# Hybrid attention and feed-forward block: pairs of projection pieces on 64-row halves of TensorE, a new order of pieces, three banks for them

## Chip, cores and metric

The kernel runs on one core of one Trainium2 chip. The metric is the device time of one launch in microseconds (us), lower is better. Times of single instructions come from one profiled execution.

## The reference

x has 8 batches of 1024 tokens with 256 features. Both branches start from the normalised x, and the output is x plus both:

```python
xn = _layernorm(x, axis=-1)
# attention branch: 16 heads of 16
x_proj = silu(xn @ W1 + b1)
u, v, q, k = split(x_proj, 4, axis=-1)
scores = einsum("bqhd,bkhd->bhqk", qh, kh)
attn = silu(scores) / S
av = einsum("bhqk,bkhd->bqhd", attn, vh).reshape(B, S, D)
y = layernorm(av * u, gamma, beta) @ W2 + b2
# feed-forward branch, ternary weights
h = layer_norm(xn, ln1_g, ln1_b) @ ternary(w1).T + b1
h = layer_norm(gelu(h), ln2_g, ln2_b)
out = h @ ternary(w2).T + b2
x = x + y + out
```

There is no softmax: each score only goes through silu, so ScalarE evaluates 8 x 16 x 1024 x 1024 of them.

## The kernel before

**Blocks, groups, rounds.** A batch is a block (b = 0 to 7). Its attention is cut into 64 groups: 2 halves c of the heads, 2 halves h of the query tokens, 2 interleaved sets o of heads, 8 tiles t of keys. A group is four score products (`scores`, line 1079), each of 64 rows and 512 columns; two of them at a time stand on the two row halves of the array. ScalarE turns a group into attn in two Silu instructions of 128x1024 (line 636), and TensorE multiplies attn by V (`times_v`, line 1101, four column tiles of 32, each fp32 product in two passes, so 8 matmul records a group). Two groups make a round; a block has 32 rounds. The text calls the 16 matmul records of line 1101 in a round "the AV products"; a round is counted from the start of its AV products to the start of the next.

**What TensorE does in a round** (`body`, line 1222): the four scores of group 2n; the AV products of the two groups before; the four scores of group 2n+1; then the pieces that the table gives the round. The first scores of a half group wait for the Silu of the same half of the group before, since there is one set of four score banks.

**Pieces.** All other TensorE work is cut into pieces, each filling one PSUM bank: `xt` (transposes of normalised x), `k`, `q`, `u` (projections, 6 matmuls of 128x512, line 1136; fp32r high and low parts), `v` (12 of 128x256), `f1.t.half` (first feed-forward product, 4 of 128x512, line 1154), `g.t.half` (4 transposes of the hidden rows, line 1163), `f2.t` (second product, 16 of 128x256, line 1170), `zt` (8 transposes in a pair of pieces, line 1180) and `a` (12 of 128x256, line 1186) for the end of the attention branch. VectorE or ScalarE empties the bank. Steps with no TensorE work stand in the same table: `gelu` (ScalarE, line 681, with a table load before and after), `ln2`, `nrm2`, `y`, `px`, `zs`, `ln1`, `xn` (VectorE), `vs` (ScalarE).

**Order.** Every engine walks the same hand-written `TABLE`, one row per group, two rows per round (line 61 and below); `LAST_ROUNDS` replaces rounds 19 to 31 in the last block. xt, k.0, q.0 and v in a row are for the next block, zt, zs and a for the one before. Pieces take the two banks `FP` in turn (`bank_of`, `turn_of`). The AV products add up in one of two banks `OP`, which change every 16 groups; VectorE reads a full one in `output` (line 831). In block 0, TensorE also computes constants (`setup_step`, line 1190) in `OP[:, 1]`.

**f2 after g.** f2.t waits with its first eight matmuls for the split of g.t.0 on VectorE (lines 917, 922 and 924), and with the other eight for g.t.1.

Of the kernel before, what the change touches and what calls it, by code (L numbers as in the profile page):

```python
# [128 lines left out]
def parsed(row):  # L129
# [9 lines left out]
    19: "ln2.2 f2.2",  # L139
# [4 lines left out]
    24: "g.5.0",  # L144
    25: "g.5.1 gelu.3 f2.5 zs.0 zt.0 zt.1",
    26: "ln2.3 a.0",
    27: "nrm2.3 g.6.0 zs.1",
    28: "g.6.1 a.1",
    29: "f2.6",
    30: "g.7.0 g.7.1",  # L150
# [75 lines left out]
def bank_of(x, step):  # L226
    return PLACE[x, step] % 2


def turn_of(x, step):  # L230
    return PLACE[x, step] // 2 + 1


def hybrid_block_kernel(nc, x, W1, b1, b1c, W2, b2, gamc, betc, l1gc, l1bc, w1T, fb1, l2gc, l2bc, w2T, fb2, out):
# [6 lines left out]
    with ctx:  # L241
# [1096 lines left out]
```

## Time and profile before

| | us |
|---|---|
| median of 3 runs | 1492.84 |
| lowest and highest | 1492.25, 1493.19 |
| the profiled execution, whole | 1493.36 |
| its span in the trace | 1491.6 |
| TensorE busy | 1464.8 (98%) |
| ScalarE busy | 1208.9 (81%) |
| VectorE busy | 895.3 (60%) |

The 1.8 us between the span and the whole lie around the span. Busy TensorE means that some matmul is in flight, not that columns stream. So the length of a round is read from starts of matmuls, and compared with what its pieces need.

### The profile page before, as it was taken

The numbers are of one execution on the slowest core, as the hardware profiler recorded it, in microseconds if no ns is written. First come the engines' busy times: TensorE is split into PE (matmuls) and PEld (weight loads), VectorE is DVE, ScalarE is ACT, GpSimd is POOL, SyncE is SP. The second block draws the span as 40 slices with busy tenths as digits, with TensorE's granted clock in tenths as the row PEclk, the third lists the DMA queues.
The fourth block names the chain that finished last, engine by engine and source line by source line (L and its number), as shares of the span: only waits on it lengthen the run. The fifth ranks groups of instructions, "written<-read, shape, count | busy, mean of one in ns | idle before, by whom it ended". The sixth has DMA issues, their size and how long they took to land.

```text
span 1491.6 us, 25963 instructions
## 1 busy us (share of the span) xinstructions
PE 1464.8 (98%) x9942; PEld 784.7 (53%) x9942; DVE 895.3 (60%) x1719; ACT 1208.9 (81%) x1273; POOL 97.4 (7%) x197
## 2 busy tenths in 40 slices
PE   8999999999999999999999999999999999999998
PEld 7445555455554555554554455545555455554544
DVE  5557655576546854468654685447755476545745
ACT  4788888888788887887878878788788887888885
POOL 2001000010000100001000010000100001000001
PEclk9999999999999999999999999999999999999999
DMA  7351052410524106340153402443033510435100
GB/s 248 81 128 57 15 132 65 130 57 15 156 71 100 58 15 156 95 104 29 30 155 99 113 1 59 126 129 84 1 89 110 142 57 5 115 81 142 29 1 29
DMA packets 67996, 123.49 MB, mean 83 GB/s; under 512 B 12832, under 2 KB 14496, under 8 KB 66976
## 3 DMA queue, kind: packets, MB, share of 16 engines
q1 hardware_dynamic: 67712, 121.57, 29.9%
q8 instruction: 79, 1.29, 0.4%
q14 instruction: 45, 0.37, 0.1%
q10 hardware_dynamic: 160, 0.26, 0.1%
HBM read 79.84 MB, written 41.94 MB: 82 GB/s over the span
## 4 chain that ended last, share of the span: by engine, by line
PE 88%; DVE 5%; ACT 4%; issue 1%; DVEq 1%; DMA 0%; ACTq 0%
PE outs L1101 30%; PE scores L1079 22%; PE fill L1136 10%; PE fill L1170 9%; PE fill L1154 7%; PE fill L1186 3%; PE fill L1163 3%; ACT attn L636 3%; PE fill L1145 2%; DVE tmp L917 1%; PE fill L1126 1%; DVE hid L900 1%; ACT hid L681 1%; DVE st L813 1%; ACT L636 1%
## 5 line engine op out<-in xcount | busy, mean ns | idle before, releaser
L636 ACT ACTIVATE attn<-scores 128x1024 f32<-128x1024 f32 x1024 | 991.4, 1023 | 225.3 <-PE scores L1079 220.6
L1101 PE MATMUL outs<-attn,V 128*32 128x512 f32 x4096 | 494.3, 600 | 0.0
L1079 PE MATMUL scores<-QS,KS 64*128 64x512 f32 x2048 | 387.7, 452 | 8.3 <-ACT attn L636 7.0
L1079 PEld LDWEIGHTS scores<-QS,KS 64*128 64x128 f32 x2048 | 163.0, 184 | 300.4 <-ACT attn L636 241.5
L1101 PEld LDWEIGHTS outs<-attn,V 128*32 128x32 f32 x4096 | 107.2, 109 | 235.8 <-issue 235.1
L900 DVE SCALAR_TENSOR_TENSOR hid<-fill,ratq,fb1b 128x512 f32<-128x512 f32 x128 | 96.1, 751 | 77.6 <-PE fill L1154 72.3
L917 DVE TENSOR_TENSOR tmp<-fill,l2g 128x512 f32<-128x512 f32 x128 | 88.6, 692 | 88.6 <-PE fill L1163 81.1
L1170 PE MATMUL fill<-Wq,hgh 128*128 128x256 f32 x504 | 128.2, 292 | 2.0 <-DVE hgl L924 1.1
L1136 PE MATMUL fill<-xp,W1h 128*128 128x512 f32 x384 | 128.4, 416 | 0.5 <-DVE xp L949 0.5
L1170 PE MATMUL fill<-Wq,hgl 128*128 128x256 f32 x504 | 123.1, 282 | 0.0
L1170 PEld LDWEIGHTS fill<-Wq,hgh 128*128 128x128 f32 x504 | 95.8, 190 | 18.9 <-issue 14.6
L1170 PEld LDWEIGHTS fill<-Wq,hgl 128*128 128x128 f32 x504 | 96.1, 191 | 0.7
L571 POOL TENSOR_TENSOR rp<-mv,epst 128x2 f32<-128x2 f32 x64 | 12.6, 197 | 1281.7 <-DVE mv L817 907.9
L924 DVE TENSOR_TENSOR hgl<-tmp,hgh 128x512 fp32r<-128x512 f32 x128 | 88.6, 692 | 9.9 <-issue 0.4
L1136 PEld LDWEIGHTS fill<-xp,W1h 128*128 128x128 f32 x384 | 66.1, 188 | 36.7 <-issue 26.9
L1163 PE MATMUL fill<-ident,hid 128*128 128x128 f32 x512 | 78.4, 281 | 3.5 <-DVE hid L900 2.1
L813 DVE BATCH_NORM_STATS2 st<-hid 128x6 f32<-128x512 f32 x128 | 79.1, 681 | 2.9
L1136 PE MATMUL fill<-xp,W1l 128*128 128x512 f32 x192 | 75.4, 392 | 0.0
L1163 PEld LDWEIGHTS fill<-ident,hid 128*128 128x128 f32 x512 | 56.0, 141 | 35.4 <-issue 25.8
L1154 PE MATMUL fill<-Wq,yT 128*128 128x512 f32 x256 | 71.5, 408 | 1.0
L1154 PE MATMUL fill<-Wq,yX 128*128 128x512 f32 x256 | 71.8, 410 | 0.0
L681 ACT ACTIVATE hid<-hid 128x2048 f32<-128x2048 f32 x32 | 60.4, 1911 | 7.7 <-DVE hid L900 7.5
(138 smaller groups left out, 1349.3 us busy)
## 6 DMA issues: line engine op xcount, KB each, us to landing
QS<-q_scratch SPq DMA_DIRECT2D x254, 128.0 KB, 3.3
k_scratch<-kst SPq DMA_DIRECT2D x64, 256.0 KB
q_scratch<-qst SPq DMA_DIRECT2D x64, 256.0 KB
KS<-k_scratch SPq DMA_DIRECT2D x128, 128.0 KB, 3.2
KS<-k_scratch SPq DMA_DIRECT2D x256, 64.0 KB, 3.4
out_dram<-part SPq DMA_DIRECT2D x15, 512.0 KB, 2.6
xin<-in_x SPq DMA_DIRECT2D x7, 1024.0 KB, 5.1
xin<-in_x SPq DMA_DIRECT2D x2, 512.0 KB, 4.3
```

Of the source, the lines that this page charges most:

```text
L636: nc.scalar.activation(attn_of(g)[:, 2 * hf:2 * hf + 2, :], SP[:, 2 * hf:2 * hf + 2, :], ACT.Silu).then_inc(s_silu, 1)
L681: nc.scalar.activation(rows, rows, ACT.Gelu).then_inc(s_gelu, 1)
L813: V_.bn_stats(st[:, j, n, :] if len(views) > 1 else st[:, j, :], v)
L900: V_.scalar_tensor_tensor(out=hid_of(t)[:, cols], in0=FP[:, k, :], scalar=ratq[:, t:t + 1], in1=fb1b[:, cols], op0=ALU.mult, op1=ALU.add). ...
L917: V_.tensor_tensor(tmp[:, :].rearrange("p (c n) -> p c n", n=P), FP[:, k, :].rearrange("p (c n) -> p c n", n=P), l2g[:, 4 * r:4 * r + 4].u ...
L924: V_.tensor_tensor(hgl[:, r, :], tmp[:, :], hgh[:, r, :].bitcast(F32), ALU.subtract).then_inc(s_hg, 1)
L1079: ins = mm(SP[:, j, :], KS[rows, pair, t * P:(t + 1) * P], QS[rows, pair - c * PPC, h * HALF:(h + 1) * HALF], start=True, stop=True)
L1101: ins = mm(OP[32 * j:32 * j + 32, g // RUN % 2, :], V[:, t, c * HPC // 2 + j, o * DH:o * DH + 2 * DH], attn_of(g)[:, n, :], start=(o == 0 ...
L1136: ins = mm(bank.rearrange("p (i n) -> p i n", i=2), w[:, kc, col:col + P], xp[:, 2 * h:2 * h + 2, part, kc, :], start=n == 0, stop=n == le ...
L1154: ins = mm(bank, y_of(t // 2)[:, part, kc, t % 2 * P:(t % 2 + 1) * P], Wq1[:, kc, hf * HALF:(hf + 1) * HALF], start=n == 0, stop=n == len( ...
L1163: ins = nc.tensor.transpose(bank[:, n * P:(n + 1) * P], hid_of(t)[:, col:col + P], ident[:, :])
L1170: ins = mm(bank[:, 0:D], w[:, r, n * P:(n + 1) * P], Wq2[:, 4 * r + n, :], start=i == 0, stop=i == len(passes) - 1)
```

## The change

1. `paired`: when the pieces of a round are exactly one pair (k and q of one half, two u, two f1 of one tile, two g of one tile), they run on 64-row halves (`in_halves`). A 128-row matmul becomes two of 64 rows, one on each row half, at the same time for different pieces. k, q, u and f1 are `crossed`: in phase 0 the first piece uses rows 0 to 63 and the second rows 64 to 127; in phase 1 they change over and add to the same banks. Before phase 1 TensorE waits for the semaphore `first_halves_done`, which the last matmul of phase 0 raises. g in halves are transposes of 64 rows. f2 stays on the full array (`SUM_IN_HALVES = False`).
2. In such a round the first half of the next group's scores stands between phase 0 and phase 1, and the second half behind phase 1. ScalarE's Silu of the first half stands before the evacuation of the pieces, the other behind it.
3. `TABLE` and `LAST_ROUNDS` are new. Blocks 1 to 6 have six rounds in halves: 2 (k.1.0 q.1.0), 6 (u.1.0 u.0.0), 9 (k.1.1 q.1.1), 10 (f1.0.0 f1.0.1), 24 and 30 (k and q of the next block). Over the kernel there are 38 such rounds of k, q or u, 8 of f1 and 4 of g (rounds 20, 22, 27, 29 of the last block).
4. Pieces have three banks; the AV products have one (`OP`). Their first product of every 16 groups waits until VectorE has read the sum before. The constants of block 0 use the third bank of the pieces; block 0 has no pieces in its first five rounds, and k.1.0 and q.1.0 run in its round 5 (`DELAYED`).
5. f2.t whose g pieces ran in halves waits for both splits before its first matmul.

```diff
-FP = ctx.enter_context(nc.psum_tensor("fill", [P, 2, HALF], F32))
+OP = ctx.enter_context(nc.psum_tensor("outs", [P, HALF], F32))
+FP = ctx.enter_context(nc.psum_tensor("fill", [P, FILLS, HALF], F32))
...
+def paired(pieces):
+
+    kinds = [s[0] for x, s in pieces]
+    if kinds == ["f2"]:
+        return SUM_IN_HALVES
+    if len(pieces) != 2 or pieces[0][0] != pieces[1][0]:
+        return False
+    (_, one), (_, two) = pieces
+    return kinds in (["f1", "f1"], ["g", "g"]) and one[1] == two[1] or kinds == ["k", "q"] and one[1:] == two[1:] or kinds == ["u", "u"]
...
+            def crossed(steps, phase):
+
+                if phase == 0:
+                    for x, step in steps:
+                        wait_free(x, step)
+                        wait_data(x, step)
+                else:
+                    pe.wait_ge(s_half, CROSSED.index(steps[0]) + 1)
+                count = 4 if steps[0][1][0] == "f1" else 6
+                for n in range(count):
+                    for half in range(2):
+                        x, step = steps[half ^ phase]
...
+                        rows = slice(half * P // 2, (half + 1) * P // 2)
...
             def body(b):
                 for n in range(ROUNDS):
-                    scores(b, 2 * n)
+                    full, group = pieces_of(b, n)
+                    nb, ng = next_group(b, 2 * n + 1)
                     for g in (2 * n - 2, 2 * n - 1):
...
-                    scores(b, 2 * n + 1)
-                    for x, s in steps_of(b, n):
+                    for hf in range(2):
+                        scores(b, 2 * n + 1, hf)
...
+                    for x, s in full:
                         step(x, *s)
...
+                    for hf in range(2):
+                        if group:
+                            in_halves(group, hf)
+                        if nb < NB:
+                            scores(nb, ng, hf)
```

Two rows of the new table that matter, rounds 25 and 26: before, "g.5.0 | g.5.1 gelu.3 v.0 xn.3 v.1 | f2.5 | ln2.3 | xt.3 v.2" reach from round 24 to 26; now round 25 is "g.5.0 g.5.1 v.0 gelu.3 v.1 xt.2 ln2.3" and round 26 "xn.3 nrm2.3 v.2 f2.5". Likewise round 15 gives up f1.6.1 and ln2.1 to round 16.

TensorE, round 24 (in block 0), before: from the scores of the odd group to the AV products of round 25. `W1h` and `W1l` are the projection weights, `xp` the transposed x.

```order
267 L1079 MATMUL scores<-QS,KS 128x512 x4
268 L1101 MATMUL outs<-attn,V 32x512 x8
269 L1079 MATMUL scores<-QS,KS 128x512 x4
270 L1136 MATMUL fill<-xp,W1h 128x512 x2
271 L1136 MATMUL fill<-xp,W1l 128x512
272 L1136 MATMUL fill<-xp,W1h 128x512 x2
273 L1136 MATMUL fill<-xp,W1l 128x512
274 L1163 MATMUL fill<-ident,hid_61 128x128 x4
275 L1079 MATMUL scores<-QS,KS 128x512 x4
276 L1101 MATMUL outs<-attn,V 32x512 x8
```

The same round in the changed kernel.

```order
272 L1165 MATMUL outs<-attn,V 32x512 x8
273 L1147 MATMUL scores<-QS,KS 128x512 x4
274 L1216 MATMUL fill<-xp,W1h 128x512 x4
275 L1216 MATMUL fill<-xp,W1l 128x512 x2
276 L1216 MATMUL fill<-xp,W1h 128x512 x4
277 L1216 MATMUL fill<-xp,W1l 128x512 x2
278 L1147 MATMUL scores<-QS,KS 128x512 x2
279 L1216 MATMUL fill<-xp,W1h 128x512 x4
280 L1216 MATMUL fill<-xp,W1l 128x512 x2
281 L1216 MATMUL fill<-xp,W1h 128x512 x4
282 L1216 MATMUL fill<-xp,W1l 128x512 x2
283 L1147 MATMUL scores<-QS,KS 128x512 x2
```

One k piece and one g piece became a k and a q piece, 24 matmuls of 64 rows, with two scores in their middle and two at their end.

ScalarE, rounds 24 to 27 of the same block, before. Line 636 is the Silu of the scores, 681 is gelu, 662 the high part of xt, 642 evacuates k or q.

```order
47 L642 ACTIVATE kst<-fill,b1s 128x512
48 L636 ACTIVATE attn<-scores 128x1024 x4
49 L681 ACT_TABLE_LOAD
50 L681 ACTIVATE hid_62<-hid_62 128x2048
51 L636 ACT_TABLE_LOAD
52 L636 ACTIVATE attn<-scores 128x1024 x4
53 L662 ACTIVATE xp<-fill 128x512
```

The same stretch in the changed kernel.

```order
43 L685 ACTIVATE kst<-fill,b1s 128x512
44 L685 ACTIVATE qst<-fill,b1s 128x512
45 L679 ACTIVATE attn<-scores 128x1024 x3
46 L724 ACT_TABLE_LOAD
47 L724 ACTIVATE hid_62<-hid_62 128x2048
48 L705 ACTIVATE xp<-fill 128x512
49 L679 ACT_TABLE_LOAD
50 L679 ACTIVATE attn<-scores 128x1024 x8
```

xt.2 moved in between gelu.3 and the table load that brings Silu back.

TensorE, round 20 of the last block, in the changed kernel: g.3.0 and g.3.1 in halves, and behind them f2.3, whose first matmul is the row of line 1319.

```order
2814 L1165 MATMUL outs<-attn,V 32x512 x8
2815 L1147 MATMUL scores<-QS,KS 128x512 x4
2816 L1235 MATMUL fill<-ident,hid_64 128x64 x8
2817 L1147 MATMUL scores<-QS,KS 128x512 x2
2818 L1235 MATMUL fill<-ident,hid_64 128x64 x8
2819 L1147 MATMUL scores<-QS,KS 128x512 x2
2820 L1165 MATMUL outs<-attn,V 32x512 x8
2821 L1147 MATMUL scores<-QS,KS 128x512 x4
2822 L1319 MATMUL fill<-Wq_57,hgh 128x256
```

Before, the same eight transposes stood in one row, ahead of all four scores:

```order
2795 L1101 MATMUL outs<-attn,V 32x512 x8
2796 L1079 MATMUL scores<-QS,KS 128x512 x4
2797 L1163 MATMUL fill<-ident,hid_64 128x128 x8
2798 L1079 MATMUL scores<-QS,KS 128x512 x4
2799 L1101 MATMUL outs<-attn,V 32x512 x8
```

The second half of the transposes now stands behind two scores, so both g banks fill at the end of the round.

## Rows read from the trace of the kernel before

**Rows 1.** The page: busy time of each engine with its share.

```profile
PE 1464.8 (98%) x9942; PEld 784.7 (53%) x9942; DVE 895.3 (60%) x1719; ACT 1208.9 (81%) x1273; POOL 97.4 (7%) x197
```

**Rows 2.** Waits, whole kernel: who waited for whom, us, times, longest.

```profile
PEld scores L1079 <- ACT attn L636: 241.5, 348, 1.3
```

**Rows 3.** Stretches: length, busy us (count) by engine, PEclk; block 5 rounds 0-10, 11-18, 19-23, 24-31.

```profile
944.19:1001.49 57.30, 56.95 (x382) 28.86 (x380) 28.19 (x60) 48.13 (x56) 3.58 (x8) 1.00 0.38 102
1001.49:1051.08 49.59, 49.06 (x310) 25.21 (x308) 35.70 (x70) 41.89 (x40) 1.79 (x5) 1.00 0.34 87
1051.08:1077.81 26.73, 26.04 (x198) 13.97 (x196) 19.14 (x35) 20.68 (x24) 5.15 (x9) 1.00 0.01 2
1077.81:1125.15 47.34, 47.25 (x343) 27.31 (x341) 26.67 (x46) 39.41 (x44) 0.89 (x2) 1.00 0.36 99
```

**Rows 4.** Stretches: block 5 rounds 11-12, 15-16, 24-26; block 0 rounds 1-10; block 7 19-31.

```profile
1001.49:1015.61 14.12, 13.98 (x78) 6.98 (x76) 8.96 (x16) 12.30 (x12) 0.00 (x0) 1.00 0.66 153
1025.29:1041.45 16.16, 15.77 (x107) 9.60 (x105) 10.94 (x20) 13.92 (x13) 0.58 (x2) 1.00 0.44 130
1077.81:1097.15 19.34, 19.25 (x144) 11.78 (x142) 11.82 (x22) 17.31 (x19) 0.89 (x2) 1.00 0.10 28
...
38.20:95.30 57.10, 57.10 (x329) 26.39 (x327) 28.34 (x47) 43.51 (x51) 0.00 (x0) 0.96 0.37 97
...
1413.09:1480.75 67.66, 63.68 (x470) 32.25 (x468) 37.98 (x74) 53.40 (x55) 3.58 (x8) 1.00 0.02 9
```

**Rows 5.** Timeline, TensorE, block 5 round 5, u.1.1 and u.1.0: start, us, line, tiles, count.

```profile
969.10 1.92 PE L1101 MATMUL outs<-attn,V 128*32 128x512 f32 x16
970.95 0.73 PE L1079 MATMUL scores<-QS,KS 64*128 64x512 f32 x4
971.62 0.73 PE L1136 MATMUL fill<-xp,W1h 128*128 128x512 f32 x2
972.19 0.39 PE L1136 MATMUL fill<-xp,W1l 128*128 128x512 f32 x1
972.42 0.63 PE L1136 MATMUL fill<-xp,W1h 128*128 128x512 f32 x2
972.88 0.39 PE L1136 MATMUL fill<-xp,W1l 128*128 128x512 f32 x1
...
974.56 0.73 PE L1079 MATMUL scores<-QS,KS 64*128 64x512 f32 x4
```

**Rows 6.** Timeline, ScalarE, the evacuation of u.1.1 in that round.

```profile
973.33 0.69 ACT L642 ACTIVATE uz<-fill,b1s 128x512 f32<-128x512 f32 x1
```

**Rows 7.** Timeline, TensorE, block 5 round 0, then ScalarE in it.

```profile
946.04 0.73 PE L1079 MATMUL scores<-QS,KS 64*128 64x512 f32 x4
946.71 1.09 PE L1180 MATMUL fill<-ident,uz 128*128 128x128 f32 x8
...
948.58 0.49 PE L1079 MATMUL scores<-QS,KS 64*128 64x512 f32 x2 [0.35 <-ACT attn L636]
949.00 1.92 PE L1101 MATMUL outs<-attn,V 128*32 128x512 f32 x16
...
946.59 3.77 ACT L636 ACTIVATE attn<-scores 128x1024 f32<-128x1024 f32 x4 [0.48 <-PE scores L1079]
```

**Rows 8.** Timeline, ScalarE, block 5: the gelu window of round 15.

```profile
1029.65 1.28 ACT L681 ACT_TABLE_LOAD   x1
1030.95 3.71 ACT L681 ACTIVATE hid<-hid 128x2048 f32<-128x2048 f32 x2
```

**Rows 9.** Timeline, TensorE, block 5 round 21: the first matmul of f2.3, the scores behind f2.3.

```profile
1064.10 0.38 PE L1170 MATMUL fill<-Wq,hgh 128*128 128x256 f32 x1
...
1066.21 0.73 PE L1079 MATMUL scores<-QS,KS 64*128 64x512 f32 x4
```

**Rows 10.** Timeline, VectorE, round 20: the split of g.3.0, the begin of g.3.1's.

```profile
1059.59 0.69 DVE L917 TENSOR_TENSOR tmp<-fill,l2g 128x512 f32<-128x512 f32 x1 [1.35 <-PE fill L1163]
...
1061.65 0.69 DVE L917 TENSOR_TENSOR tmp<-fill,l2g 128x512 f32<-128x512 f32 x1
```

More of the change, by code:

```diff
@@ L138 @@
 LAST_ROUNDS = {
-    19: "ln2.2 f2.2",
+    19: "f2.2",
     20: "g.3.0 g.3.1 nrm2.2",
@@ L143 @@
     23: "f2.4",
[L144 to L150, printed above, removed]
+    24: "",
+    25: "g.5.0 g.5.1 gelu.3 ln2.3 zs.0 zt.0 zt.1",
+    26: "nrm2.3 f2.5 a.0",
+    27: "g.6.0 g.6.1 zs.1",
+    28: "f2.6 a.1",
+    29: "g.7.0 g.7.1",
+    30: "",
     31: "",
@@ L164 @@
 assert sorted(OPENING) == sorted(s for s in ORDER if is_next(s))
-EARLIER = {1: parsed("k.1.0")}
-MOVED = [s for n in sorted(EARLIER) for s in EARLIER[n]]
+SETUP_ROUNDS = 5
+DELAYED = [s for g in range(2 * SETUP_ROUNDS) for s in SLOTS[g] if s[0] in FILLERS and s[0] not in POST and not is_next(s)]
 def steps_of(b, n):
@@ L176, in steps_of @@
         return
-    if b == 0:
-        for s in EARLIER.get(n, ()):
-            yield b, s
+    if b == 0 and n == SETUP_ROUNDS:
+        for s in DELAYED:
+            yield 0, s
     for g in (2 * n, 2 * n + 1):
@@ L431, in last_piece @@
         def last_piece(bank):
-            return [xs for xs in PIECES if bank_of(*xs) == bank][-1]
+            return [xs for xs in PIECES if bank in [k for k, turn in BANKS[xs]]][-1]
         def last_a_tile(i, j):
@@ L730, in _ @@
                         sum_of_abs(i)
+            for hf in range(2):
+                silu_half(0, 0, hf)
+            act.wait_ge(s_const, 3)
+            step(0, "vs", 0)
             for b in range(NB):
@@ new lines, in transposed @@
+            def transposed(steps, phase):
+                if phase == 0:
+                    for x, step in steps:
+                        wait_free(x, step)
+                        wait_data(x, step)
+                for c in range(phase * HC // 2, (phase + 1) * HC // 2):
+                    for half in range(2):
+                        x, (kind, t, r) = steps[half]
+                        k = bank_of(x, (kind, t, r))
+                        toks = slice(half * P // 2, (half + 1) * P // 2)
+                        ins = nc.tensor.transpose(FP[:, k, c * P // 2:(c + 1) * P // 2], hid_of(t)[toks, c * P:(c + 1) * P],
+                                                  ident[toks, toks])
+                        if c == HC - 1:
+                            ins.then_inc(s_fill[k], 1)
@@ new lines, in summed @@
+            def summed(steps, phase):
+                (x, step), = steps
+                t = step[1]
+                if phase == 0:
+                    wait_free(x, step)
+                pe.wait_ge(s_hg, 2 * T * x + 2 * t + 2)
+                for n in range(4):
+                    for w in (hgh, hgl):
+                        for half, (k, turn) in enumerate(BANKS[x, step]):
+                            rows = slice(half * P // 2, (half + 1) * P // 2)
+                            ins = mm(FP[:, k, 0:D], w[rows, phase, n * P:(n + 1) * P], Wq2[rows, 4 * phase + n, :],
+                                     start=phase == 0 and n == 0 and w is hgh, stop=phase == 1 and n == 3 and w is hgl)
+                            if phase == 1 and n == 3 and w is hgl:
+                                ins.then_inc(s_fill[k], 1)
@@ L1110, in step, with in_halves @@
+            def in_halves(steps, phase):
+                kind = steps[0][1][0]
+                (transposed if kind == "g" else summed if kind == "f2" else crossed)(steps, phase)
             def step(x, kind, *a):
@@ L1280, in _ @@
                 step(0, *s)
+            for hf in range(2):
+                scores(0, 0, hf)
             for b in range(NB):
                 body(b)
-            pe.wait_ge(s_z, DC * NH * (NB - 1) + 3)
+            wait_evacuated(pe, *last_piece(2))
             last_hidden(0)
```

308 lines of the change are left out of this document (193 added, 115 removed).

## The prediction

> **What bounds the kernel now.** The busy times come first: TensorE 98%, ScalarE 81%, VectorE 60% [rows 1]. A busy TensorE only has a matmul in flight, so next comes who waits. TensorE's weight loads for the scores wait 348 times for a Silu, 241.5 us in all, mostly while matmuls still run [rows 2]; ScalarE is a second bound close behind. Which of the two sets a round is read from starts.
>
> In round 5 of block 5 TensorE is the bound [rows 5]. AV products to scores 1.85; a block of scores 0.67 (970.95 to 971.62); one 512-column matmul 0.23 (972.19 to 972.42). The first two full matmuls take 0.57, so entering the full array costs 0.11; a score block is two pairs, 0.46, plus 0.21 for coming and going. A change of tile shape costs about 0.20 in all. So a round needs 1.85 + 0.67 + 0.66 = 3.18, plus 0.20 for any full pieces, plus the pieces: k, q or u 6 x 0.23 = 1.38, f1 0.92; f2 (2.11 - 0.20)/16 = 0.12 a matmul, 1.91 in all, v and a 1.43 [rows 9]; g, zt and xt some 0.11 a transpose, 0.43 [rows 7]. Check: round 5 with two u gives 6.14; measured 974.56 + 0.67 - 969.10 = 6.13.
>
> In round 0 the Silus are the bound [rows 7]: the first starts 0.55 after its scores, two take 1.95, and only then may the last scores go (the 0.35 of waiting), 0.42 ahead of the next AV products. 1.85 + 0.55 + 1.95 + 0.05 + 0.42 = 4.82: no round is shorter, and one piece of k, q, u, a or f1 is free in it.
>
> **A round in halves.** From its scores to the next AV products all stands on 64-row tiles, so two changes of shape go, 0.40. I take 0.23 for two 64-row matmuls side by side, since the score block shows 0.23 a pair. The wait for `first_halves_done` is new and no row shows it. Nearest: the last matmul of u.1.1 starts at 972.88 [rows 5], ScalarE begins on its bank at 973.33 [rows 6], 0.45 later. Between the phases stands one score pair, so phase 1 is due 0.46 after the last start of phase 0: the signal comes just in time, but weights are not loaded ahead, which costs the 0.10 of an entry. Bounds 0 and 0.34 (an entry and a whole matmul); I take 0.10, as the signal is on time. Behind this wait on TensorE are the second scores and the AV products. Round: 1.85 + 0.34 + 0.23 x (12 + 2) + 0.33 + 0.10 = 5.84 for two of k, q, u, against 6.13 in full; 4.92 for two f1, against 5.2. ScalarE evacuates both pieces at the end of such a round and ahead of a Silu (2 x 0.6, then 0.97), done some 2.1 after the AV products begin; the scores that need it are due at 2.19. It hides.
>
> **Middle blocks, by stage** (before: [rows 3]).
> - Rounds 0 to 10: round 0 has four zt, 3.38 + 1.72 + 0.15 (the fourth waits for the first bank, behind `output` on VectorE) = 5.25; three in halves 17.52; f1 4.92; six at the floor 28.92. Sum 56.6 against 57.30: -0.7.
> - Rounds 11 to 18: the gelu windows decide. A window on ScalarE starts 4.36 after the AV products, and a load, one gelu, a load are 4.5, two gelus 6.4 [rows 8]. Round 11: the even group's Silus begin at 8.87 instead of 9.8, since f1.1.1 is now the second piece. The next odd scores wait for them until 10.87, another floor's rest (0.55 is hidden, so 1.95 + 0.42) gives rounds 11 and 12 13.2 against 14.12 [rows 4]. Rounds 15 and 16: Silus at 10.80 both before and after. Round 15 now has TensorE work for only 8.9, round 16 for 6.20 instead of 5.28 (f1.6.1 moved out of the window). The odd scores of 16 wait until 12.8, then 0.33 + 0.10 + 2.83 + 0.76 give 16.8 against 16.16 [rows 4]. Four rounds at the floor: 49.2 against 49.6: -0.4.
> - Rounds 19 to 23: with a third bank xt need not wait for g's evacuation. Rounds 20 and 22 fall to the floor 4.82, three f2 rounds are 3.38 + 1.91 = 5.29 each. 25.5 against 26.73: -1.2.
> - Rounds 24 to 31: 5.84 for 24. Round 25: the window is 4.5 as before, and the copy of xt.2 now stands in it (0.6), so the even Silus begin at 9.45. TensorE has work for only 7.6 there; f2.5 went to 26. The odd scores wait until 11.44, then 0.33 + 0.10 + 3.34 + 0.76: 15.9 for 25 and 26. Rounds 24 to 26: 21.7 against 19.34 [rows 4]. Rounds 27 to 31: 4.82, 5.29, 5.66, 5.84 + 0.4 (vs.0, 1.15 on ScalarE, delays a Silu into round 30), 5.29: 27.3 against 28.0. Together 49.0 against 47.34: +1.7.
>
> Sum -0.6 to -0.7 a block, six blocks: **-4.2**.
>
> **Block 0 and the opening.** v.2 no longer waits for a bank, -0.4. Rounds 1 to 10 [rows 4]: k.1.0 leaves round 1 (-1.2), where the granted clock is still low in places (0.96 over the stretch), and q.1.0 and k.1.0 fill rounds in halves later (5.84 + 5.84 + 4.82 + 4.82 + 5.84 + 4.92 = 32.1; rounds 5 to 10 took 6.13 with two u and one k, q or u in a floor of 4.82 in most others, some 31.2; +0.9). The setup's wait before the first piece in round 5 is for a VectorE step of round 4 and hides. The remaining stages cancel. **-0.6**.
>
> **Last block.** Rounds 0 to 18: -1.1. From 19 on [rows 4], 67.66 before. Four g pairs run in halves; both banks fill at the end of the round, some 4.5 after its AV products. VectorE needs 2.06 for a split [rows 10], two run one behind the other, so g.1's is ready at 8.5, that is 3.65 into the next round; f2 is due at 2.6. Three f2 follow such a round (21, 23, 28): +1.05 each, 3.1; round 22 and 20 stay at the floor, so nothing is gained for it. f2.5 leaves the gelu window and a.0 waits for zs.0 behind ln2.3 on VectorE: 25 and 26 take 15.35 against 13.6, +1.8. f2.6 and a.1 share round 28 (6.71) and round 30 stands empty at 4.82: +1.1. **+6.0**, so +4.9 for the block.
>
> **The single `OP` bank:** `output` starts when the AV products of rounds 8, 16, 24, 0 end and VectorE is then done within 3.7 of the round's start (12.6 after round 15 starts, where round 17 starts at 16.8). It hides under scores and pieces; if VectorE were 4 us late, each of 31 sums would hold TensorE.
>
> **Sum:** -4.2 - 0.6 + 4.9 = +0.1. Against the profiled execution's 1493.36 that is 1493.5; the median is 0.5 lower: **1493**.
>
> **Rivals.**
> - *Forecast*, the halves' gain is given back in the gelu windows and the last block: 1490 to 1496, chance 0.42.
> - *A, faster:* the phase change costs nothing. 46 crossed rounds x 0.10 = 4.6: 1488.5. For it: the signal at 0.45 against 0.46; against: a weight load behind a wait is not ahead anywhere in the rows. 0.14.
> - *B, faster:* the windows cost less, because ScalarE's chain gives way (TensorE idles 1.65 in rounds 15 and 16 and 1.65 in 25 and 26 by my count; before it was 1.1 and 0.4). If these stay as before, 1.8 x 7 blocks = 12.6: 1480; half of it 1487. Against: Silus and loads are in program order. 0.17.
> - *C, slower:* a pair on halves takes more than 0.23, as two weight loads must go by for each. 520 pairs; at 0.25 +10.4: 1503. It decides from 0.236 on. Against: the score block's 0.67. For: the score block has only two pairs, and never shows a third. 0.14.
> - *D, slower:* the phase change costs the upper bound, 0.34: 46 x 0.24 = +11: 1504. 0.10.
> - *E:* the halves run one after the other, a pair 0.46: +120, 1613. The scores run side by side in 0.67 where one after the other would take 1.13. 0.02.
>
> On C the Trainium skill has a rule that speaks against this change: "TensorEngine Tiling (Array Packing)", Instruction Overhead, states some 60 cycles of overhead for each matmul. Halving adds 520 matmuls; an estimate from that page is 520 x 25 ns = 13 us, a time of 1506. The score block above does not show such an overhead. On the pace, "TensorE: Matmul & The Clock Gate", in Wait — 56ns, not 53.3ns?, has 215.7 ns from start to start for 512 columns at full clock; the row has 0.23, so the row is used. If only the halves kept the page's pace, its 14 ns on 520 pairs would be an estimate of 7 us less, which lies within A and B.
>
> **Range and chances.** What is left out is E and the outer parts of B, C and D: 1483 to 1503. About 3 us (0.2%) is what a measurement here can tell from no change. Below 1490: A, B and a little of the forecast, 0.32. Within: 0.40. Above 1496: C, D, E and the forecast's edge, 0.28.
>
> **What would show it.** In the changed profile: rounds 2, 6, 9, 24, 30 at 5.84 and 10 at 4.92 (starts of AV products); starts of 64-row pairs 0.23 apart, 0.56 from the last of phase 0 to the first of phase 1 with the scores between; rounds 20 and 22 at 4.82; 15 with 16 near 16.8, 25 with 26 near 15.9, with TensorE idle for Silus there; rounds 21 and 23 of the last block near 6.3, with a wait for hgl. It is wrong if pairs are not 0.23 apart, if `output` shows up as a waiter's cause, or if a full round with three pieces still waits for a bank.

## Result, and the profile after

The changed kernel takes **1505.79 us** (median of 7 runs, 1500.05 to 1510.05), against 1492.97 (1492.25 to 1493.19, 7 runs) for the kernel before beside it: ratio 1.008, 95% interval 1.0062 to 1.0098. Slower by 0.8%, where no change was forecast, and above the range that was given. The profiled execution is the one of 1507.53, its span 1505.7 us, against 1491.6 before; what follows accounts for the difference of these two spans. Blocks, rounds and stretches are counted as before.

The busy times on the page of the changed kernel (compare [rows 1]):

```profile
PE 1458.3 (97%) x10494; PEld 802.4 (53%) x10494; DVE 894.8 (59%) x1719; ACT 1205.7 (80%) x1273; POOL 98.1 (7%) x197
```

TensorE has a matmul in flight for 6.5 us less than before and yet the span is 14 us longer, so it stands still for some 20 us more. For whom, the waits say (engine and line, what it waited for, us in total, times, longest); first a row of the kernel before, then two of the changed one:

```profile
PE scores L1079 <- ACT attn L636: 7.0, 17, 1.1
...
PE scores L1147 <- ACT attn L679: 34.2, 54, 2.8
...
PE fill L1319 <- DVE hgl L981: 3.2, 3, 1.1
```

The weight loads wait for the Silus as long as before (242.5 us in all, against [rows 2]), which costs nothing while matmuls run. TensorE itself is idle until a Silu is done for 34.2 us where it was 7.0. The last row is three waits of f2 for `hgl`; before, there was one of 1.1.

Stretches of the changed kernel (length, busy us and count by engine, PEclk, share of DMA, GB/s). First block 5's rounds 0 to 10, 11 to 18, 19 to 23, 24 to 31, the rows that answer to [rows 3]; then rounds 16 and 26 of block 5, and round 16 of block 3; last rounds 25 and 26 of block 7.

```profile
945.10:1002.48 57.38, 57.16 (x432) 29.89 (x430) 27.67 (x60) 48.97 (x55) 3.56 (x8) 1.00 0.39 107
1002.48:1053.20 50.72, 48.94 (x307) 26.60 (x305) 35.74 (x70) 40.94 (x39) 3.18 (x6) 0.97 0.37 104
1053.20:1078.71 25.51, 25.51 (x194) 13.73 (x193) 18.84 (x34) 20.04 (x23) 3.74 (x8) 1.00 0.01 2
1078.71:1129.35 50.64, 49.33 (x371) 29.65 (x369) 27.39 (x48) 39.75 (x44) 0.89 (x2) 0.97 0.28 69
...
1034.18:1043.56 9.38, 8.07 (x47) 5.23 (x45) 7.42 (x14) 5.60 (x7) 0.89 (x2) 0.82 0.22 84
1092.18:1102.05 9.87, 8.56 (x55) 5.99 (x54) 8.17 (x15) 5.61 (x7) 0.89 (x2) 0.83 0.88 218
...
670.20:678.06 7.86, 6.54 (x47) 3.80 (x45) 7.01 (x14) 5.62 (x7) 0.86 (x2) 1.00 0.21 88
...
1450.35:1467.34 16.99, 13.76 (x95) 8.71 (x93) 12.01 (x27) 11.66 (x12) 3.23 (x6) 0.90 0.00 0
```

Two stretches of block 5 have a PEclk of 0.97 where before every one had 1.00. It sits in one round each: round 16 takes 9.38 at 0.82, and the same round of block 3, at 1.00, 7.86. The granted clock is at its full level, 2.4 GHz, up to there, then for a part of the round at the lower one, 1.2 GHz. In the kernel before this happened in the opening alone, and behind the last matmul. In this execution it happens five times more: round 26 of block 3, rounds 16 and 26 of block 5, rounds 26 and 31 of block 7. Each costs what the round is longer than its undisturbed twin: 1.52 (9.38 - 7.86), in two rounds 1.49 (9.87 - 8.38), in round 31 1.67 (5.34 against 3.67 in two runs below without this fall). Round 26 of block 7 has no undisturbed twin; an estimate from the row above (PEclk 0.90 over 17 us) is 0.10 x 17 = 1.7. Together 7.9 us.

What the engine does ahead of a fall stands in round 26 of block 3. Timeline of TensorE, then of ScalarE (start, us, engine, line, tiles, count, idle time before and its cause):

```profile
726.67 1.92 PE L1165 MATMUL outs<-attn,V 128*32 128x512 f32 x16
729.49 0.50 PE L1147 MATMUL scores<-QS,KS 64*128 64x512 f32 x2 [0.89 <-ACT attn L679]
730.40 0.51 PE L1147 MATMUL scores<-QS,KS 64*128 64x512 f32 x2 [0.42 <-ACT attn L679]
...
732.73 0.41 PE L1319 MATMUL fill<-Wq,hgh 128*128 128x256 f32 x1
732.94 0.41 PE L1319 MATMUL fill<-Wq,hgl 128*128 128x256 f32 x1
...
735.55 0.28 PE L1319 MATMUL fill<-Wq,hgh 128*128 128x256 f32 x1
735.67 0.28 PE L1319 MATMUL fill<-Wq,hgl 128*128 128x256 f32 x1
```

```profile
724.70 1.92 ACT L724 ACTIVATE hid<-hid 128x2048 f32<-128x2048 f32 x1
726.52 0.58 ACT L705 ACTIVATE xp<-fill 128x512 fp32r<-128x512 f32 x1
727.12 1.28 ACT L679 ACT_TABLE_LOAD   x1
728.41 3.77 ACT L679 ACTIVATE attn<-scores 128x1024 f32<-128x1024 f32 x4
```

ScalarE works through its window (a gelu, the copy of xt.2, a table load, two Silus); TensorE has nothing until 729.49 and again until 730.40. Then it starts on v.2 and f2.5. The clock falls in the middle of v.2, and the same f2 matmuls that later start 0.12 apart start 0.21 apart.

The round lengths in the table are those of the sum, with one exception beside the falls, round 10 (medians of blocks 1 to 6, from the starts of the AV products):

| rounds | before | forecast | after |
|---|---|---|---|
| two pieces in halves (2, 6, 9, 24) | | 5.84 | 5.86, 5.86, 5.86, 5.84 |
| 10, f1 in halves | 5.68 | 4.92 | **5.50** |
| 11 and 12 | 14.12 | 13.2 | 13.14 |
| 15 and 16, clock at 1.00 | 16.20 | 16.8 | 16.81 |
| 20, 22 | 5.21 | 4.82 | 4.82 |
| 25 and 26, clock at 1.00 | 14.12 | 15.9 | 16.00 |
| block 7: 21, 23 / 28 | 5.29, 5.28 / 5.20 | 6.34 / 7.76 | 6.37, 6.36 / 7.86 |
| block 7: 31 | 3.66 | 3.66 | **5.34** |

A round in halves, round 9 of block 3 with k and q, on TensorE:

```profile
629.59 0.63 PE L1216 MATMUL fill<-xp,W1h 64*128 64x512 f32 x4
...
630.73 0.39 PE L1216 MATMUL fill<-xp,W1l 64*128 64x512 f32 x2
630.96 0.39 PE L1147 MATMUL scores<-QS,KS 64*128 64x512 f32 x2
631.18 0.74 PE L1216 MATMUL fill<-xp,W1h 64*128 64x512 f32 x4
631.76 0.40 PE L1216 MATMUL fill<-xp,W1l 64*128 64x512 f32 x2
```

Pairs start 0.23 apart (630.73, 630.96, 631.18). The wait between the phases shows in the first of the second phase: its two pairs take 0.58 (631.18 to 631.76) instead of 0.46, so 0.12.

Round 10 of block 3, TensorE and then VectorE:

```profile
635.91 1.18 PE L1209 MATMUL fill<-Wq,yT 64*128 64x512 f32 x8 [0.19 <-issue]
```

```profile
625.11 2.29 DVE L929 TENSOR_TENSOR part<-xin,cst 128x2048 f32<-128x2048 f32 x1
...
635.12 0.69 DVE L945 TENSOR_TENSOR yT<-tmp,yT 128x512 fp32r<-128x512 f32 x1
```

f1.0.0 could go at 635.55, behind the scores of round 10 (634.88 + 0.67); it starts at 635.91, 0.10 after the last step of y.0 (635.12 + 0.69). Ahead of y.0 VectorE has px (2.29), y.2 and y.1 in a row from 625.11 on, all of them in round 8 of the table. In blocks 6 and 7 y.0 is done later still, and round 10 takes 5.85 and 5.88.

### The profile page after: what moved, and what is told of

It is laid out like the page before. It is cut to its first block, busy times and chain, and to the rows that moved or that the text cites. A ratio compares the mean times of both kernels' runs of the same rounds, so it can differ in the third digit from the quotient of the medians.

```text
span 1505.7 us, 27163 instructions
## 1 busy us (share of the span) xinstructions
PE 1458.3 (97%) x10494; PEld 802.4 (53%) x10494; DVE 894.8 (59%) x1719; ACT 1205.7 (80%) x1273; POOL 98.1 (7%) x197
## 4 chain that ended last, share of the span: by engine, by line
PE 82%; ACT 16%; DVE 1%; issue 1%; DMA 0%; DVEq 0%; ACTq 0%
PE outs L1165 28%; PE scores L1147 21%; PE fill L1319 8%; PE fill L1216 7%; ACT attn L679 7%; ACT hid L724 4%; PE fill L1303 3%; PE fill L1335 3%; PE fill L1312 3%; PE fill L1285 2%; ACT L679 2%; ACT L724 2%; PE fill L1294 2%; PE fill L1209 1%; PE fill L1329 1%; PE fill L1275 1%
## 5 line engine op out<-in xcount | busy, mean ns | idle before, releaser
L1147 PE MATMUL scores<-QS,KS 64*128 64x512 f32 x2048 | 401.4, 454 | 35.0 <-ACT attn L679 34.2
L1147 PEld LDWEIGHTS scores<-QS,KS 64*128 64x128 f32 x2048 | 170.7, 184 | 329.2 <-ACT attn L679 242.5
L983 DVE TENSOR_TENSOR tmp<-fill,l2g 128x512 f32<-128x512 f32 x120 | 83.0, 691 | 63.8 <-PE fill L1312 56.3
L1216 PE MATMUL fill<-xp,W1h 64*128 64x512 f32 x608 | 99.3, 404 | 0.0
L891 DVE SCALAR_TENSOR_TENSOR uz<-outs,uz 128x512 f32<-128x512 f32 x31 | 21.3, 689 | 126.1 <-PE outs L1165 126.1
L990 DVE TENSOR_TENSOR hgl<-tmp,hgh 128x512 fp32r<-128x512 f32 x120 | 83.1, 692 | 9.0
L1312 PE MATMUL fill<-ident,hid 128*128 128x128 f32 x480 | 68.6, 278 | 0.0
L1023 DVE CAST kst<-kst 128x512 fp32r<-128x512 f32 x32 | 13.7, 427 | 89.9 <-ACT kst L685 89.2
L1216 PEld LDWEIGHTS fill<-xp,W1h 64*128 64x128 f32 x608 | 54.3, 184 | 19.3 <-PE fill L1216 9.8
L996 DVE SCALAR_TENSOR_TENSOR part<-fill,cq,part 128x256 f32<-128x256 f32 x63 | 30.5, 484 | 56.6 <-PE fill L1319 52.0
```

The source lines that it names most:

```text
L983: V_.tensor_tensor(tmp[:, :].rearrange("p (c n) -> p c n", n=P), FP[:, k, :].rearrange("p (c n) -> p c n", n=P), l2g[:, 4 * r:4 * r + 4].u ...
L990: V_.tensor_tensor(hgl[:, r, :], tmp[:, :], hgh[:, r, :].bitcast(F32), ALU.subtract).then_inc(s_hg, 1)
L1147: ins = mm(SP[:, j, :], KS[rows, pair, t * P:(t + 1) * P], QS[rows, pair - c * PPC, h * HALF:(h + 1) * HALF], start=True, stop=True)
L1216: ins = mm(FP[:, k, :].rearrange("p (i n) -> p i n", i=2), w[rows, kc, col:col + P], xp[rows, 2 * h:2 * h + 2, part, kc, :], start=phase = ...
L1312: ins = nc.tensor.transpose(bank[:, n * P:(n + 1) * P], hid_of(t)[:, col:col + P], ident[:, :])
```

## Experiments

Every kernel is compared with new runs of the kernel before on the same chip: 1492.73 us (1492.17 to 1493.5) for clock_kept to old_table, 1492.98 (1492.03 to 1493.47) for windows_filled to mixed, 1492.93 for mixed_full. "Falls" are stretches of lower granted clock inside the blocks, of the profiled execution. All ratios are to the kernel before, with 95% intervals.

| kernel | us (runs) | ratio | span | falls |
|---|---|---|---|---|
| changed | 1505.79 (7) | 1.008 [1.0062, 1.0098] | 1505.7 | 5 |
| clock_kept | 1502.67 (4) | 1.0064 [1.0049, 1.0079] | 1499.9 | 2 |
| y_early | 1500.32 (5) | 1.0042 [1.0028, 1.0056] | 1501.9 | 5 |
| full_array | 1510.91 (4) | 1.0122 [1.0107, 1.0137] | 1509.3 | 4 |
| old_table | 1489.05 (7) | 0.9974 [0.9963, 0.9985] | 1486.4 | 0 |
| windows_filled | 1495.02 (10) | 1.0012 [1.0003, 1.0021] | 1491.2 | 1 |
| g_full | 1507.53 (4) | 1.0092 [1.007, 1.0115] | 1509.0 | 9 |
| old_ln2_late | 1486.13 (5) | 0.9955 [0.9942, 0.9967] | 1484.6 | 0 |
| mixed | **1471.4** (4) | **0.9856** [0.9843, 0.987] | 1470.2 | 0 |
| mixed_full | 1478.02 (4) | 0.9903 [0.9887, 0.992] | 1476.1 | 0 |

**Clock kept up.** Six products of the identity go ahead of the odd scores of rounds 16 and 26, into the bank of the next piece, which overwrites them.

```diff
+            def keep_busy(xs):
+
+                wait_free(*xs)
+                for _ in range(6):
+                    mm(FP[:, bank_of(*xs), 0:P], ident[:, :], ident[:, :], start=True, stop=True)
...
+                    if n in (16, 26):
+                        keep_busy(full[0])
```

> The changed kernel with six 128-column matmuls of the identity put in TensorE's idle time in rounds 16 and 26 of each block, between the AV products and the odd scores; they write the bank of the next piece, which overwrites it. Theory: the granted clock falls to half for a stretch because TensorE idles there (0.89 and 0.42 us one after the other), and each fall costs 1.5 to 1.7. Then no fall is left in these rounds, rounds 16 stay near 7.9 and 26 near 8.4 in every block, and the time is near the fastest run of the changed kernel, 1499 to 1501, with a spread of 1 to 2 us; one fall at the end of the last block (round 31) may stay. Rival, the falls have another cause: the clock falls as before in some rounds 16 and 26, the time stays spread over 1500 to 1510, median near 1506.

Rounds 16 and 26 of block 5 (same columns as above):

```profile
1031.54:1039.37 7.83, 7.83 (x59) 5.22 (x57) 6.97 (x14) 5.69 (x7) 0.84 (x2) 1.00 0.24 96
1087.97:1096.35 8.38, 8.38 (x67) 5.92 (x65) 7.48 (x14) 5.72 (x7) 0.89 (x2) 1.00 0.87 209
```

TensorE does useless work in the same wait, the rounds take 7.83 and 8.38, and the clock falls in no round of blocks 0 to 6; the two falls left are in rounds 26 and 31 of block 7. Round 30, ahead of 31, has no products of the identity. Round 26 has them, but its wait is longer (2.82 in the changed kernel), and 1.28 of it stay idle:

```profile
1451.53 1.60 PE L1178 MATMUL fill<-ident 128*128 128x128 f32 x12
1454.42 0.49 PE L1147 MATMUL scores<-QS,KS 64*128 64x512 f32 x2 [1.28 <-ACT attn L679]
```

The runs spread over 1.3 us instead of 10. The idle time ahead brings the falls about, and the same wait with the clock up costs what the sum said. The median, 1502.67, is above the 1499 to 1501 expected: it keeps the fall of round 31, which three of the changed kernel's runs, at 1500.05 to 1502.04 and a mean clock of 0.997, may not have.

**y earlier.** px and y.2 go one round earlier.

```diff
-    "u.1.1",
-    "px u.0.1 y.2",
+    "u.1.1 px y.2",
+    "u.0.1",
```

> The changed kernel with px and y.2 moved from round 8 to round 7. Theory: round 10 takes 5.5 instead of 5.0 because f1.0.0 waits for y.0, which VectorE reaches late behind px, y.2 and y.1; the move takes 0.45 to 0.55 off round 10 in eight blocks, 4 us: near 1501.5 as a median, with the clock falls in rounds 16 and 26 left. Rival, the 0.5 of round 10 is a cost of the halves (f1 pairs slower, or the phase change): round 10 stays at 5.5 and the time stays at 1506.

Round 10 of block 3:

```profile
634.94:640.01 5.07, 5.07 (x43) 2.54 (x41) 2.33 (x5) 4.81 (x6) 0.00 (x0) 1.00 0.19 40
```

Round 10 becomes 5.07 in every block, from about 5.50 in six and 5.85 and 5.88 in the last two, 4.1 us in all, at an unchanged number of falls; the spans differ by 3.8. VectorE's queue held up f1.0.0. The 0.15 that are left over 4.92 show no wait: TensorE has a matmul in flight throughout. Their cause stays open.

**All on the full array.** No pair in halves, order and banks as changed.

```diff
 def paired(pieces):
 
+    return False
```

> The changed kernel with no round in halves: same table, same three banks, all pieces on the full array. Theory: a round of two k, q or u takes 6.13 instead of 5.86 (38 rounds, +10), round 10 stays near 5.5, and the last block loses the waits of f2 behind g in halves (3 x -1.05): 1512 to 1514. Rival, halves bring nothing: 1503 to 1506.

Rounds 2 and 10 of block 5:

```profile
963.09:969.21 6.12, 6.12 (x38) 3.19 (x36) 2.28 (x7) 4.85 (x6) 1.25 (x3) 1.00 0.25 56
1005.57:1010.92 5.35, 5.26 (x34) 2.51 (x32) 4.70 (x10) 4.09 (x6) 0.00 (x0) 1.00 0.04 8
```

6.12 against 5.86 with halves. The median is 5.1 above the changed kernel's, so the halves are not where the time went. The median also lies 1.1 below the expected range. Since the clock falls a different number of times in each run, the gain of the halves is read better in the last pair of kernels below.

**The old order in the new code.** `TABLE`, `LAST_ROUNDS` of the kernel before, with three banks for pieces and one for AV products; only rounds 5 and 6, and three g rounds of the last block, run in halves. Two places of the edit:

```diff
-    "f2.0 g.1.0 gelu.1 gelu.2 f1.6.0 g.1.1",
-    "",
-    "ln2.1 f1.6.1 f2.1",
+    "f1.5.0 f2.0 f1.5.1",
+    "gelu.1 f1.6.0 g.1.0 gelu.2 g.1.1 ln2.1 f1.6.1",
...
-    25: "g.5.0 g.5.1 gelu.3 ln2.3 zs.0 zt.0 zt.1",
-    26: "nrm2.3 f2.5 a.0",
+    25: "g.5.1 gelu.3 f2.5 zs.0 zt.0 zt.1",
+    26: "ln2.3 a.0",
```

> The changed kernel with the table and last rounds of the kernel before: three banks, one bank for the AV products, and halves only where the old table happens to have a pair alone (rounds 5 and 6 of each block, rounds 20, 22 and 30 of the last). Theory: the loss of the changed kernel comes from its order alone. Here two rounds of 6.13 become 5.86, rounds 20 and 22 fall from 5.21 to 4.82, rounds 11, 15 and 25 lose 0.3 each, k.1.0 leaves round 1 of block 0, and the clock stays up because TensorE is not idle in rounds 16 and 26: about -2.2 a block, near 1477, between 1473 and 1483. Rival, the halves or the single bank for the AV products cost time: 1493 or more.

It is 3.7 us faster than the kernel before, far less than expected. Rounds 15 and 16 of block 5, the first AV products of round 17 on TensorE, VectorE ahead of them, and the waits of this kind in the whole kernel:

```profile
1017.87:1034.83 16.96, 15.73 (x106) 9.81 (x105) 11.64 (x21) 14.90 (x14) 0.89 (x2) 1.00 0.42 125
```

```profile
1034.83 1.49 PE L1165 MATMUL outs<-attn,V 128*32 128x512 f32 x12 [1.01 <-DVE uz L891]
```

```profile
1030.41 2.47 DVE L867 BATCH_NORM_STATS2 st<-hid 128x6 f32<-128x512 f32 x4
1032.96 0.28 DVE L871 BATCH_NORM_AGGREGATE mv<-st 128x2 f32<-128x12 f32 x2
1033.33 0.75 DVE L954 SCALAR_TENSOR_TENSOR hid<-fill,ratq,fb1b 128x512 f32<-128x512 f32 x1
1034.00 0.68 DVE L891 SCALAR_TENSOR_TENSOR uz<-outs,uz 128x512 f32<-128x512 f32 x1
```

```profile
PE outs L1165 <- DVE uz L891: 8.1, 8, 1.0
```

L891 empties the AV bank. It stands behind ln2.1 (2.47 + 0.28) and f1.6.1's evacuation, and with a single bank the next AV products wait for it: 8 times in the kernel, 8.1 us. That is the price of giving the third bank to the pieces, in this order; the changed order has ln2.1 behind L891 there and doesn't pay it. In the last block the g pairs in halves cost 1.07 to 1.08 in each of rounds 21, 23 and 31 (6.36, 6.35 and 4.74 against 5.29, 5.28 and 3.66), 3.2. The two together are 11.3 us, about what is missing from the expected 1477. There are no falls.

**The windows filled.** In the changed order, f1.6.1 goes to round 15 and f2.5 to round 25.

```diff
-    "f2.0 g.1.0 gelu.1 gelu.2 f1.6.0 g.1.1",
+    "f2.0 g.1.0 gelu.1 gelu.2 f1.6.0 g.1.1 f1.6.1",
...
-    "ln2.1 f1.6.1 f2.1",
+    "ln2.1 f2.1",
...
-    "g.5.0 g.5.1 v.0 gelu.3 v.1 xt.2 ln2.3",
+    "g.5.0 g.5.1 v.0 gelu.3 v.1 xt.2 f2.5 ln2.3",
...
-    "xn.3 nrm2.3 v.2 f2.5",
+    "xn.3 nrm2.3 v.2",
```

> The changed kernel with f1.6.1 moved from round 16 to round 15 and f2.5 from round 26 back to round 25, so that TensorE has a piece to run while ScalarE computes Silus. Theory 1 (the two Silu windows of the changed order leave TensorE without work, and that both costs time itself and lets the granted clock fall afterwards): rounds 15+16 together 16.2 us instead of 16.8, rounds 25+26 about 14.6 instead of 16.0 (the kernel before has 14.1 there with one piece less), so about -2.0 us a block over 7 to 8 blocks, -15; no clock falls in rounds 16 and 26 of blocks 0 to 6, -3 to -5 more; the last block, whose own rows are as they were, keeps its falls. Time about 1486, 1483 to 1490. Theory 2 (the windows are as long as ScalarE's chain of Silus and Exps, whatever TensorE has to do): 16.8 and 16.0 stay, only the clock falls go: 1501 to 1503.

Rounds 15 with 16 and 25 with 26 of block 5; then f2.5 in round 25 on TensorE, and VectorE before it:

```profile
1018.53:1034.40 15.87, 15.46 (x106) 9.73 (x104) 10.95 (x18) 13.80 (x13) 0.00 (x0) 1.00 0.45 133
1075.37:1091.24 15.87, 14.63 (x114) 9.81 (x112) 12.67 (x24) 13.07 (x14) 0.89 (x2) 1.00 0.59 156
```

```profile
1083.65 0.39 PE L1319 MATMUL fill<-Wq,hgh 128*128 128x256 f32 x1 [1.24 <-DVE vraw L1033]
```

```profile
1082.05 0.69 DVE L990 TENSOR_TENSOR hgl<-tmp,hgh 128x512 fp32r<-128x512 f32 x1
...
1082.91 1.52 DVE L1033 TENSOR_TENSOR vraw<-fill,bvb 128x512 f32<-128x512 f32 x2 [0.16 <-issue]
```

The first window behaves as expected, and better: 0.94 less than 16.81. The second doesn't: 15.87, not 14.6. TensorE again idles 1.24, no longer for a Silu but for the bank which v.0 still holds: it starts 0.05 after the first of the two instructions of L1033 is done (1083.60). VectorE comes to that evacuation only behind the splits of both g.5 pieces, the second of them done at 1082.74 (1082.05 + 0.69). The order itself holds this up: with k.0.0 and q.0.0 paired in round 24, both g.5 stand in round 25. The clock falls in no round of blocks 0 to 6 of the profiled execution, as expected, though TensorE idles 1.24 in a row. The runs lie at 1492.91 to 1493.22 with a mean clock of 0.996 to 0.997 and at 1494.88 to 1496.15 with 0.994 to 0.995, so other executions have a fall or two more, where isn't known. The median misses the 1483 to 1490 expected; it is 10.8 us faster than the changed kernel.

**g on the full array.** Only the four g pairs of the last block.

```diff
-    return kinds in (["f1", "f1"], ["g", "g"]) and one[1] == two[1] or kinds == ["k", "q"] and one[1:] == two[1:] or kinds == ["u", "u"]
+    return kinds == ["f1", "f1"] and one[1] == two[1] or kinds == ["k", "q"] and one[1:] == two[1:] or kinds == ["u", "u"]
```

> The changed kernel with the g pairs of the last block (rounds 20, 22, 27, 29) on the full array again; all other halves stay. Theory (halved g delays both Silu inputs, and the f2 piece of the next round waits for ScalarE and VectorE behind them): rounds 21 and 23 fall from 6.36 to 5.29, round 28 from 7.86 to 6.75, round 31 from 5.34 to 3.66 since f2.7 and its clock fall go with it; together -4.9, time about 1500.5 (1497 to 1503, since the falls of the clock elsewhere vary from run to run). Rival: the waits belong to the order of f2 against g, not to the halves: within 1 us of 1505.8.

Rounds 21 and 23 take 5.29 and 5.28, round 28 takes 6.72: the mechanism is as told for these three. Round 31 takes 3.67, but windows_filled, with g in halves and no fall there, has 3.67 as well, so in round 31 it is the clock and not g. The time did not follow, since in the profiled execution the clock fell nine times, in round 16 or 26 of blocks 2 to 7. Round 26 of block 5 takes 9.87 again.

By the runs: 1500.55 at a mean granted clock of 0.994, 1505.95 at 0.991, 1509.1 at 0.988, 1510.74 at 0.986. One kernel, ten us apart. The changed kernel's runs lie the same way: 1500.05 to 1502.04 at 0.997, 1505.79 at 0.993, 1507.5 to 1507.8 at 0.992, 1510.05 at 0.990.

**The old order with ln2.1 later.** Against old_table; g is on the full array, with the edit of g_full.

```diff
-    "gelu.1 f1.6.0 g.1.0 gelu.2 g.1.1 ln2.1 f1.6.1",
-    "nrm2.1",
-    "f2.1",
-    "g.2.0 f1.7.0",
+    "gelu.1 f1.6.0 g.1.0 gelu.2 g.1.1 f1.6.1",
+    "",
+    "ln2.1 f2.1",
+    "nrm2.1 g.2.0 f1.7.0",
```

> The kernel with the old table of steps in the new code (1489.05), now with ln2.1 one round later (16, beside f2.1) and nrm2.1 in round 17, and the last block's g pairs on the full array. Theory (with a single bank for the AV products, round 17's products wait 0.99 us until VectorE has taken round 16's output, which stands behind ln2.1 and f1.6.1): rounds 15+16 fall from 16.95 to about 16.0, -1.0 in each of 8 blocks, -7.6; the g pairs -1.07 in rounds 21 and 23 and -1.1 in round 31, -3.2: about 1478 (1476 to 1481). Rival (the 0.76 us of rounds 15+16 against the kernel before come from three banks for the pieces, or from ScalarE): only the g part comes, 1486.

Rounds 15 with 16, then 17, of block 3, and g.2.0 in round 17 on TensorE:

```profile
658.97:674.83 15.86, 15.63 (x107) 9.76 (x105) 10.72 (x18) 13.81 (x13) 0.00 (x0) 1.00 0.46 133
674.83:680.75 5.92, 4.73 (x34) 2.07 (x32) 4.20 (x9) 3.87 (x5) 0.89 (x2) 1.00 0.00 0
```

```profile
678.60 0.63 PE L1312 MATMUL fill<-ident,hid 128*128 128x128 f32 x4 [1.19 <-DVE hid L966]
```

The wait for L891 is gone and 1.10 with it, as expected. But nrm2.1 went a round later too, g.2.0 stands ahead of f1.7.0 on TensorE and waits 1.19 for it: round 17 takes 5.92 instead of 4.82. A wait was moved, not removed; only the last block's 3 us came.

**Mixed.** Rounds 0 to 18 in the changed order, with the two edits on y and f1.6.1; rounds 19 to 31 and the last block in the old one; g on the full array. f1.7.0 stands ahead of g.2.0 here. The third bank for pieces and the single one for AV products stay.

> Rounds 0 to 18 in the changed order (with halves in rounds 2, 6, 9, 10), px and y.2 one round earlier and f1.6.1 in round 15 as in the two experiments on these; rounds 19 to 31 and the last block in the old order; the last block's g pairs on the full array. Theory (each of the parts adds up): rounds 0 to 10 56.9 us as measured with px early, 11 to 14 22.8, 15+16 about 16.1, 17+18 9.6, 19 to 31 73.2 as measured with the old table: 178.6 a block against 180.2, -13, and -3 in the last block: about 1474 (1471 to 1478), and no clock falls but the opening's. Rival (the early piece in round 15 doesn't fill the window, and the clock falls in round 16 of some blocks): 1480 to 1486.

Block 5's rounds 0 to 10, 11 to 18, 19 to 23, 24 to 31 (against [rows 3] and the stretches above):

```profile
929.64:986.62 56.98, 56.98 (x431) 29.88 (x429) 27.72 (x60) 48.77 (x56) 3.56 (x8) 1.00 0.33 90
986.62:1034.91 48.29, 47.36 (x306) 25.02 (x304) 35.71 (x70) 41.05 (x40) 3.17 (x6) 1.00 0.42 105
1034.91:1060.87 25.96, 25.96 (x199) 14.13 (x197) 19.59 (x36) 20.48 (x24) 3.74 (x8) 1.00 0.01 2
1060.87:1108.09 47.22, 47.22 (x342) 27.31 (x340) 26.67 (x46) 39.41 (x44) 0.89 (x2) 1.00 0.36 100
```

178.4 us a block, no fall and 1471.4 us: 21.6 less than before, 34 less than the changed kernel. Against the changed kernel's undisturbed blocks, rounds 0 to 10 gain 0.4, 11 to 18 0.9, and 24 to 31 1.9 (49.1 to 47.2), while 19 to 23 give back 0.45.

**Mixed, all on the full array.** `paired` returns False, as above.

> The mixed kernel (1471.4) with every pair on the full array: order, banks and waits as they were. Theory (where nothing else is late, halves are worth what the round lengths show, 5.86 against 6.12): rounds 2, 6 and 9 +0.26 each and round 10 +0.1 to +0.3, so +0.9 a block, +7 in all: about 1478.5 (1477 to 1480), the granted clock unchanged. Rival (halves gain nothing beyond the order, since ScalarE or the waits between the two phases take it back): within 1 us of 1471.4.

Block 5's rounds 0 to 10 and 11 to 18:

```profile
932.73:990.52 57.79, 57.79 (x386) 29.55 (x385) 28.95 (x61) 48.20 (x56) 3.58 (x8) 1.00 0.32 93
990.52:1038.79 48.27, 47.35 (x307) 25.01 (x305) 34.51 (x69) 41.75 (x40) 3.18 (x6) 1.00 0.39 98
```

0.81 more in rounds 0 to 10, where the pairs are, 0.02 less in 11 to 18, 6.6 us in all. The four rounds with pairs have 0.18 to 0.26 more each; round 3, behind the pair of round 2, has 0.10 less (4.82 against 4.92). So of mixed's 21.6, halves are 6.6 and the rest, order and banks together, 15.0; no run takes these two apart. Neither kernel has a fall inside the blocks; only the opening's stretch at the lower clock differs between executions, which in these two profiles is 1.35 us in round 1 of block 0 (7.71 and 6.36).

## Why the prediction was wrong, step by step

**Right.** The round's own model, with a round in halves (5.84, measured 5.84 to 5.86); the wait between the phases (0.10, measured 0.12), so rivals A and D fall; the pace of pairs (0.23), so C falls, and E with it. The estimate from Instruction Overhead in "TensorEngine Tiling (Array Packing)" of the Trainium skill falls too: mixed has 352 matmuls more than mixed_full (10294 against 9942) and is 6.6 us shorter. That the measured 1505.79 lies at that estimate's 1506 is chance. The three windows (13.2, 16.8 and 15.9, measured 13.14, 16.81 and 16.00), so B falls. It is the move of f1.6.1 out of round 15 that costs there: with the piece back in it, the window takes 15.87 (windows_filled). The gain in rounds 20 and 22, the +1.05 of f2 behind halved g (1.07; g_full takes it away), and the AV bank, which costs nothing in the changed order, but 1.0 a block as soon as ln2.1 stands ahead of it (old_table). None of the prediction's three signs of being wrong appeared; they covered only terms that stood in the sum.

**Wrong, the main part: a term that was missing.** The sum counted the idle of TensorE in rounds 16 and 26 as lost time (1.65 us each by its count, 1.31 in the trace) and rival B named it, but the step stopped there. Idle has a second price here: the granted clock may fall to the lower level behind it, 1.5 to 1.7 us each time, five times in the profiled execution, 7.9 of the 14.1 us. The one trace at hand had falls in the opening alone (PEclk 0.96 in [rows 4]), and nothing asked what the new idle stretches, 0.89 and 0.42, would do. clock_kept shows the cause, the undisturbed twins of the rounds the size. On the clock the Trainium skill has a passage that fits: "TensorE: Matmul & The Clock Gate", A second HAM failure mode: psum-queue depth-cycling, tells of a kernel whose short idles between groups of matmuls let the clock go up and down. The rows here agree: in blocks 0 to 6 the falls come behind idles under 1 us. It would have been ground for one more rival, though no row of the kernel before had a price for it.

**Wrong, the second part: round 10.** "f1 4.92" took TensorE's work for granted and never asked when y.0 would be ready. px, y.2, y.1 and y.0 in one round are 10.7 us of VectorE (625.11 to 635.81), and with f1 first behind them round 10 takes 5.50 in six blocks and 5.85 and 5.88 in two, together 5.3 above the sum. y_early takes 4.1 of it back; the other 1.2 (0.15 a block) is the round's own length, sized too low.

**Wrong in size.** Rounds 0 to 10 have 0.02 more in each round in halves and 0.10 in round 3 on top of round 10. The prediction's own four stages add up to -0.6 a block, so to -3.6 for six blocks and not -4.2, a slip of 0.6 that changes nothing. The last block's rounds 19 to 31 gave back 9.4 us (77.1 against 67.7), of which 3.4 are its two falls; the 6.0 left are the forecast. Its rounds 0 to 18 came out even, where the sum had -1.1: round 10 again, at 5.88.

**The sum again.** Forecast +0.1; falls 7.9; round 10 5.3; some 0.8 of small terms: +14.1, the difference of the two spans (1505.7 and 1491.6).

**What stays open.** Why the clock falls in some of these rounds and not in others of the same execution: the 14 rounds 16 and 26 of blocks 0 to 6 have nearly the same idles, and the clock fell in three of them in one profile and in eight in that of g_full. And why a single idle of 1.24 (windows_filled), 1.19 (old_ln2_late) or 1.01 (old_table) was never followed by a fall in the profiles, while 0.89 with 0.42 was, at times. No run places idles of one length apart, and none changes the banks alone.

## What to carry to other kernels

Pairing pieces on halves of the array pays what the saved changes of tile shape are worth, here 0.26 us a pair of k, q or u, once the order leaves nothing else late; judge order and halves apart, since one change here moved both, and the halves' 6.6 us (mixed against mixed_full) were lost in the rest of it. When a change makes a saturated TensorE idle for even a microsecond near a long ScalarE chain, price the idle twice, once as time and once as a possible fall of the clock, and take several runs, as such a kernel spreads over 10 us. And for each step moved, ask on every engine's own queue what now stands ahead of it: three of the misses here (y.0, ln2.1 ahead of the AV bank's evacuation, nrm2.1) were one in-order queue each.

## What was not expected of the hardware

- The granted clock fell to half after idles of 0.89 and 0.42 us (in one round 2.82 and 0.41) in a TensorE that is 97% busy, in five places of one profiled execution and in nine of a near twin's; each of the five cost 1.5 to 1.7 us.
- Six matmuls without use in that wait kept the clock up in all 14 such rounds of a profile, at no cost in round time (7.83 and 8.38). In a wait that left 1.28 and 0.42 idle, the clock fell all the same.
- Two 64-row matmuls side by side start every 0.23 us, as one 128-row matmul does, in phases of four or six pairs; the added wait for the other phase cost 0.12.
